# Queueing the routing stage of a transformer block behind the iterations of its local attention

## What is computed

```
xn   = layernorm(x)
s    = xn @ [q_route_tok, kv_route_tok]      # 2 rows of 2048 scores
for 20 rounds:                               # per row
    a = cur * (log k - logsumexp((s + b) / cur))
    b = -relu(s + a);  cur = max(0.7 * cur, 0.03)
idx_q, idx_kv = top_k(exp((s + a + b) / cur), 1024)
light = local_attention(layernorm(xn))       # 8 heads, windows of 64, look-around 1
heavy = attention(tokens idx_q over tokens idx_kv)
x = x + light + scatter(heavy, idx_q; null token elsewhere)
x = x + mixture_of_8_experts_top2(layernorm(x))
```

## Time and profile before

| | |
|---|---|
| median of 3 runs | 8584.27 us (8556.19 to 8604.47) |
| profiled execution | 8584.97 us |
| its span on the slowest core (core 4) | 8583.4 us |
| spans of the eight cores | 8517.4 to 8583.4 us |
| PE, DVE, ACT, POOL busy | 5417.4, 3297.1, 1409.5, 305.0 us |
| TensorE clock granted, mean of core 4 | 0.743 of full speed |

### The profile page before, as it was taken

The page is one execution under the profiler, slowest core; times in us unless marked ns, Lnnn a source line. Parts: engine busy times, 40 slices in busy tenths (PEclk is TensorE's granted clock), DMA queues, the critical chain, the costliest instruction groups (busy, mean ns, idle before and its releaser), DMA issues.

```text
span 8583.4 us, 70890 instructions; the slowest of 8 cores (8517.4 to 8583.4 us)
## 1 busy us (share of the span) xinstructions
PE 5417.4 (63%) x21893; PEld 2079.2 (24%) x22208; DVE 3297.1 (38%) x5936; ACT 1409.5 (16%) x1819; POOL 305.0 (4%) x335
## 2 busy tenths in 40 slices
PE   5220122245555445561698888888988888888887
PEld 1010000013333333310232332322323223232232
DVE  2733644484444444425332332333333333232232
ACT  1012000102222222210111111111111111111111
POOL 0022000000000000000000000000000000000000
PEclk8565555566555555575897998989989999897898
DMA  2110000010000000010211111112111020211110
GB/s 91 44 10 0 0 0 0 5 44 6 1 1 1 1 1 1 1 49 0 37 24 17 29 30 16 31 15 31 29 18 31 16 31 16 31 16 30 16 31 40
DMA packets 149539, 169.20 MB, mean 20 GB/s; under 512 B 55972, under 2 KB 125092, under 8 KB 142772
## 3 DMA queue, kind: packets, MB, share of 16 engines
q0 software_dynamic: 140512, 111.61, 8.8%
q1 hardware_dynamic: 8660, 53.04, 1.8%
HBM read 267.67 MB, written 8.39 MB: 32 GB/s over the span
## 4 chain that ended last, share of the span: by engine, by line
PE 43%; DVE 4%; issue 3%; ACT 1%; DMA 1%; POOL 0%; DVEq 0%; another core or an unknown queue 0%; ACTq 0%; PEldq 0%; POOLq 0%
PE pSIM L1341 22%; PE pSIM L1415 12%; PE pSIM L1346 4%; PE pMISC L1302 2%; DVE x L1438 2%; PE pMISC L1383 2%; PE pSIM L1421 1%; ACT gtmp L1365 1%; DVE gtmp L1370 1%; DVE gTq L1376 1%; DMA b3ce<-b3c 1%; DVE u2sb L1394 0%; PE pSIM L1324 0%; DVEq L155 0%; DVE u3sb L1320 0%
## 5 line engine op out<-in xcount | busy, mean ns | idle before, releaser
L1415 PE MATMUL pSIM<-gTq,w2b 128*128 128x512 bf16 x4001 | 1196.3, 444 | 320.2 <-DVE gTq L1376 224.7
L1438 DVE SCALAR_TENSOR_TENSOR x<-pSIM,x 128x512 f32<-128x512 f32 x1024 | 708.3, 692 | 787.2 <-PE pSIM L1415 430.1
L1341 PE MATMUL pSIM<-xl2T,w1b 128*128 128x512 bf16 x3984 | 987.2, 389 | 31.0 <-DVE u3sb L1320 24.6
L1341 PE MATMUL pSIM<-xl2T,w3b 128*128 128x512 bf16 x4010 | 976.0, 383 | 4.7 <-issue 0.8
L1370 DVE TENSOR_TENSOR gtmp<-gtmp,gtmp 128x512 bf16<-128x512 bf16 x512 | 217.8, 425 | 1891.1 <-ACT gtmp L1365 1891.1
L1356 ACT ACTIVATE gtmp<-pSIM,b1ce 128x512 bf16<-128x512 f32 x512 | 351.8, 687 | 2965.9 <-PE pSIM L1346 2949.1
L1415 PEld LDWEIGHTS pSIM<-gTq,w2b 128*128 128x128 bf16 x4096 | 386.4, 108 | 1050.7 <-issue 869.6
L969 PE MATMUL pT<-idbf,attnbf 128*128 128x128 bf16 x2048 | 258.7, 306 | 592.5 <-ACT attnbf L953 567.2
L1341 PEld LDWEIGHTS pSIM<-xl2T,w1b 128*128 128x128 bf16 x4096 | 364.8, 99 | 521.9 <-issue 186.2
L1341 PEld LDWEIGHTS pSIM<-xl2T,w3b 128*128 128x128 bf16 x4096 | 360.4, 98 | 488.2 <-issue 144.2
L1365 ACT ACTIVATE gtmp<-pSIM,b3ce 128x512 bf16<-128x512 f32 x512 | 352.0, 688 | 729.2 <-PE pSIM L1346 729.2
(11 more groups left out here) (262 smaller groups left out, 4781.3 us busy)
## 6 DMA issues: line engine op xcount, KB each, us to landing
w1b<-w1q POOLq DMA_DIRECT2D x32, 1024.0 KB, 10.1
w3b<-w3q POOLq DMA_DIRECT2D x32, 1024.0 KB, 14.3
w2b<-w2q POOLq DMA_DIRECT2D x32, 1024.0 KB, 17.1
xs<-xT SPq DMA_DIRECT2D x24, 1024.0 KB, 4.9
xc<-xT SPq DMA_DIRECT2D x16, 1024.0 KB, 4.9
out<-x SPq DMA_DIRECT2D x8, 1024.0 KB, 10.2
wst<-wqkv POOLq DMA_DIRECT2D x8, 256.0 KB, 4.1
cos<-cos SPq DMA_DIRECT2D x1, 1024.0 KB
```

Of the source, the lines that this page charges most:

```text
L1341: E.matmul(pSIM[:, 512 * bank:512 * bank + 512], wb[:, 512 * dc + 128 * hc:512 * dc + 128 * hc + 128], xl2T[:, 2048 * dc + 512 * tc: 2048 ...
L1415: ins = E.matmul(pch(yb), w2b[par][:, 1024 * hc + 128 * dc: 1024 * hc + 128 * dc + 128], gTq[:, 512 * hc:512 * hc + 512], start=(hc == 0), ...
L1438: E.scalar_tensor_tensor(x1[:, 2048 * dc + 512 * tc: 2048 * dc + 512 * tc + 512], pch(yb), 1.0, x1[:, 2048 * dc + 512 * tc: 2048 * dc + 51 ...
```

## The change

The block c1 goes. Its operations are recorded as before, but between `begin_stage` and `end_stage`, which keep them in lists of their own together with the order in which they were recorded over all engines. They have semaphores of their own (c1p, c1v, c1w, c1s, c1m, c1x). After iteration `it` of c2, `feed` appends recorded operations to the engines' lists until a share of (it + 1) / 72 of them is out, so the last go out after iteration 71. The recorded list has 398 operations. The two broadcasts go through the one bank of pMISC in four pieces of 512 columns (`c1bcast`), since pSIM is in use by c2. Four tiles that lay over lightT, which c2 writes, move to the area of ln2T: kbkv, cscr, u_rt, key_rt. Ahead of the next stage, four engines wait for all of c1's semaphores. In the list below the renamed semaphores of the other c1 operations are left out.

```diff
         self.q[eng].append((w, emit, None if inc is None else inc.h, k, pend))
+        if getattr(self, "_stage_on", False):
+            self.gseq.append(eng)
...
+    def begin_stage(self, ordmap):
+        self._saveq, self._saveord = self.q, self.ord
+        self.q = {e: [] for e in ENGS}
+        self.ord = ordmap
+        self.gseq = []
+        self._stage_on = True
+
+    def end_stage(self):
+        st = self.q
+        self.q, self.ord = self._saveq, self._saveord
+        self._stage_on = False
+        return [self.gseq, st, 0]
+
+    def feed(self, stage, frac):
+        gseq, st, done = stage
+        want = int(math.ceil(len(gseq) * min(1.0, frac)))
+        while done < want:
+            e = gseq[done]
+            self.q[e].append(st[e].pop(0))
+            done += 1
+        stage[2] = done
...
-    kbkv = sat("kbkv", [128, 2048], F32, LT)
-    cscr = sat("cscr", [128, 2048], F32, LT + 8192)
+    kbkv = sat("kbkv", [128, 2048], F32, BIG + 24576)
+    cscr = sat("cscr", [128, 2048], F32, BIG + 0)
...
-    u_rt = rowt("u_rt", 0, 0, 2, 2048, F32, LT)
-    key_rt = rowt("key_rt", 0, 0, 2, 2048, F32, LT + 8192)
+    u_rt = rowt("u_rt", 0, 0, 2, 2048, F32, BIG + 16384)
+    key_rt = rowt("key_rt", 0, 0, 2, 2048, F32, BIG + 8192)
...
+    def c1bcast(src_row, dst, wait=()):
+        b = _ap_base(src_row)
+        for tc in range(4):
+            P.do("tensor", (lambda b=b, tc=tc: lambda E:
+                            E.matmul(pMISC[:, 0:512], ones_f[b:b + 1, :],
+                                     src_row[:, 512 * tc:512 * tc + 512],
+                                     start=True, stop=True))(),
+                 waits=[(S["c1s"], S["c1s"].n),
+                        (S["c1w"], S["c1w"].n)] + list(wait),
+                 inc=S["c1m"])
+            P.do("scalar", (lambda dst=dst, tc=tc: lambda E:
+                            E.copy(dst[:, 512 * tc:512 * tc + 512],
+                                   pMISC[:, 0:512]))(),
+                 waits=[(S["c1m"], S["c1m"].n)], inc=S["c1s"], drain=True)
...
         P.do("gpsimd", lambda E: E.tensor_sub(u_rt, s_rt, rl_rt),
-             waits=[(S["scl"], S["scl"].n), (S["pool"], S["pool"].n)],
-             inc=S["pool"], drain=True)
+             waits=[(S["c1s"], S["c1s"].n), (S["c1p"], S["c1p"].n)],
+             inc=S["c1p"], drain=True)
...
-    P.flush("c1")
...
+    c1stage = P.end_stage()
 
     VC2 = S["vec"].n
     for it in range(128):
...
              waits=[(S["av"], S["av"].n)], inc=S["oe"], drain=True)
+        P.feed(c1stage, (it + 1) / 72.0)
+    P.feed(c1stage, 1.0)
+    assert not any(c1stage[1].values())
     P.flush("c2")
...
+    C1F = [(S[k], S[k].n) for k in ("c1p", "c1v", "c1w", "c1s", "c1m", "c1x")]
+    for _e in ("tensor", "vector", "scalar", "gpsimd"):
+        P.do(_e, lambda E: E.nop(), waits=C1F)
     P.do("vector", lambda E: E.tensor_mul(t_row, r_row, sr_row),
          inc=S["vec"], drain=True)
```

More of the change, by code:

```diff
@@ L350, in build @@
              "scl", "scl2", "pool", "sim", "mx", "ex", "tp", "tes", "tev",
-             "av", "rr", "rb", "oe", "fin"]
-    names += ["o_vector", "o_scalar", "o_gpsimd"]
+             "av", "rr", "rb", "oe", "fin",
+             "c1p", "c1v", "c1w", "c1s", "c1m", "c1x"]
+    names += ["o_vector", "o_scalar", "o_gpsimd",
+              "c1ov", "c1os", "c1og"]
     S = {k: Sem(nc, k) for k in names}
@@ L600, in build @@
         tap("lq", lq); tap("lk", lk); tap("vsh", vsh)
+    P.begin_stage({"vector": S["c1ov"], "scalar": S["c1os"],
+                   "gpsimd": S["c1og"]})
+    def c1bcast(src_row, dst, wait=()):
[12 more added lines that the diff above has]
+                 waits=[(S["c1m"], S["c1m"].n)], inc=S["c1s"], drain=True)
     P.do("gpsimd", lambda E: E.tensor_copy(rl_rt, s_rt),
-         waits=[(S["vec"], S["vec"].n)], inc=S["pool"], drain=True)
+         waits=[(S["vec"], S["vec"].n)], inc=S["c1p"], drain=True)
     cur_eps = 4.0
@@ L608, in build @@
         P.do("gpsimd", lambda E: E.tensor_sub(u_rt, s_rt, rl_rt),
-             waits=[(S["scl"], S["scl"].n), (S["pool"], S["pool"].n)],
-             inc=S["pool"], drain=True)
+             waits=[(S["c1s"], S["c1s"].n), (S["c1p"], S["c1p"].n)],
+             inc=S["c1p"], drain=True)
         P.do("vector", lambda E: E.reduce_max(sc_rt[:, 0:1], u_rt, axis=AX.X),
-             waits=[(S["pool"], S["pool"].n)], inc=S["vec"], drain=True)
+             waits=[(S["c1p"], S["c1p"].n)], inc=S["c1v"], drain=True)
         P.do("vector", (lambda inv=inv: lambda E:
@@ L630, in build @@
                                         ALU.mult, ALU.add))(),
-             inc=S["pool"], drain=True)
+             inc=S["c1p"], drain=True)
         P.do("scalar", lambda E: E.activation(rl_rt, s_rt, AF.Relu,
                                               bias=sc_rt[:, 5:6], scale=1.0),
-             waits=[(S["pool"], S["pool"].n)], inc=S["scl"], drain=True)
+             waits=[(S["c1p"], S["c1p"].n)], inc=S["c1s"], drain=True)
         cur_eps = max(cur_eps * 0.7, 0.03)
@@ L637, in build @@
                                              ALU.add, ALU.min),
-         waits=[(S["scl"], S["scl"].n)], inc=S["pool"], drain=True)
+         waits=[(S["c1s"], S["c1s"].n)], inc=S["c1p"], drain=True)
     P.do("gpsimd", lambda E: E.tensor_scalar(z_rt, key_rt, 0.0, None, ALU.is_equal),
-         inc=S["pool"], drain=True)
-    P.do("gpsimd", lambda E: E.memset(u_rt, 1.0), inc=S["pool"], drain=True)
+         inc=S["c1p"], drain=True)
+    P.do("gpsimd", lambda E: E.memset(u_rt, 1.0), inc=S["c1p"], drain=True)
     P.do("vector", lambda E: E.tensor_tensor_scan(zp_rt, u_rt, z_rt, 0.0,
                                                   ALU.mult, ALU.add),
[L644 to L647, removed]
+         waits=[(S["c1p"], S["c1p"].n)], inc=S["c1v"], drain=True)
+    P.do("vector", lambda E: E.tensor_sub(zp_rt, zp_rt, z_rt), inc=S["c1v"], drain=True)
+    P.do("vector", lambda E: E.tensor_mul(zp_rt, zp_rt, z_rt), inc=S["c1v"], drain=True)
+    c1bcast(key_rt[0:1, :], cmpw, wait=[(S["c1v"], S["c1v"].n)])
     for c in range(16):
@@ L651, in build @@
                                     key_rt[:, 128 * c:128 * c + 128], idf[0:2, 0:2]))(),
-             waits=[(S["vec"], S["vec"].n), (S["vec2"], S["vec2"].n),
-                    (S["scl"], S["scl"].n)],
-             inc=S["mm3"])
+             waits=[(S["c1s"], S["c1s"].n), (S["c1w"], S["c1w"].n)],
+             inc=S["c1m"])
         P.do("vector", (lambda c=c: lambda E:
                         E.tensor_copy(kcol[:, 2 * c:2 * c + 2], pMISC[0:128, 0:2]))(),
-             waits=[(S["mm3"], S["mm3"].n)], inc=S["vec2"], drain=True)
+             waits=[(S["c1m"], S["c1m"].n)], inc=S["c1w"], drain=True)
     for c in range(16):
@@ L661, in build @@
                                     idf[:, :]))(),
-             waits=[(S["vec2"], S["vec2"].n)], inc=S["mm3"])
+             waits=[(S["c1w"], S["c1w"].n)], inc=S["c1m"])
         P.do("vector", (lambda c=c: lambda E:
@@ L665, in build @@
                                       pMISC[0:1, 0:128]))(),
-             waits=[(S["mm3"], S["mm3"].n)], inc=S["vec2"], drain=True)
-    bcast(t_row, kbkv, wait=[(S["vec2"], S["vec2"].n)])
+             waits=[(S["c1m"], S["c1m"].n)], inc=S["c1w"], drain=True)
+    c1bcast(t_row, kbkv, wait=[(S["c1w"], S["c1w"].n)])
     for c in range(16):
@@ L674, in build @@
                                             ALU.is_gt))(),
-                 waits=[(S["vec2"], S["vec2"].n), (S["scl"], S["scl"].n)],
+                 waits=[(S["c1w"], S["c1w"].n), (S["c1s"], S["c1s"].n)],
                  drain=True)
@@ L684, in build @@
                                     idf[:, :]))(),
-             waits=[(S["mx"], S["mx"].n), (S["vec2"], S["vec2"].n)],
-             inc=S["mm3"])
+             waits=[(S["c1x"], S["c1x"].n), (S["c1w"], S["c1w"].n)],
+             inc=S["c1m"])
         P.do("vector", (lambda c=c: lambda E:
@@ L689, in build @@
                                       pMISC[0:2, 0:128]))(),
-             waits=[(S["mm3"], S["mm3"].n)], inc=S["vec2"], drain=True)
+             waits=[(S["c1m"], S["c1m"].n)], inc=S["c1w"], drain=True)
     P.do("vector", lambda E: E.tensor_add(rank_rt, rank_rt, zp_rt),
-         waits=[(S["vec2"], S["vec2"].n)], inc=S["vec"], drain=True)
+         waits=[(S["c1w"], S["c1w"].n)], inc=S["c1v"], drain=True)
     P.do("vector", lambda E: E.tensor_scalar(sel_rt, rank_rt, 1024.0, None, ALU.is_lt),
-         inc=S["vec"], drain=True)
+         inc=S["c1v"], drain=True)
     P.do("vector", lambda E: E.tensor_scalar(nmqbf[:, :], rank_rt[0:1, :], 1024.0,
                                              None, ALU.is_ge),
-         inc=S["vec"], drain=True)
+         inc=S["c1v"], drain=True)
     for c in range(16):
@@ L701, in build @@
                                     sel_rt[:, 128 * c:128 * c + 128], idf[0:2, 0:2]))(),
-             waits=[(S["vec"], S["vec"].n), (S["vec2"], S["vec2"].n)],
-             inc=S["mm3"])
```

(15 more changed lines are left out.)

12 lines of the change are left out of this document (6 added, 6 removed).

## The result

The changed kernel takes 8469.35 us (median) against 8587.11. Some executions of either kernel are a slower kind, with one die at a lower granted clock (0.70 against 0.75 in the worst), and the ratio is taken over the others: 0.9868, 95% interval 0.9841 to 0.9895, so some 113 us less (1.3%). The slowest core of the profiled execution is core 3 now (core 4 before).

What follows compares the result with a forecast made beforehand. No engine bounds c1 or c2; each is one serial chain hopping between engines. Three stretches, to 359.5, 778.3 and 1066 us, make a stage of about 1067 against 1192: 8585 - 125 = 8460 us, range 8425 to 8520.

Steps and rivals of the forecast that it cites:

- Part 1: The 20 scoring rounds of c1 beside iterations 0 to 32 of c2: 359.5 us, overlap taking 117 off.
- the walk: Batch-by-batch queue calculation for the 20 rounds, from start distances in the old timelines; iteration 33 starts at 359.5 us.
- the lock: Rival, chance 0.33: in seven batches the GpSimd subtract holds up DVE's scaling of lattnT; 17 us, total 8477.
- s: The GpSimd subtract in each of the 20 scoring rounds, 4.66 us to the next start; the operation itself lasts 4.48.
- much over 18: Sign of a wrong prediction: a scoring round, forecast to spread over 18 us instead of 15.2, takes much longer.
- near the lower end: Forecast's choice for the subtract disturbing DVE, between bounds of nothing and +90 us over twenty rounds.
- The rival's 7 x 2.5 us: Scaling of lattnT delayed by the GpSimd subtract in batches 5, 10, 15, 18, 23, 28, 31: 17 us; chance 0.33.
- Part 2: End of c1 beside iterations 33 to 71: 195.3 and 208.8 us add up, 404 us, reaching 778.3.
- Part 3: Iterations 72 to 127 of c2 alone: 56 x 5.14 = 287.8 us, reaching 1066.
- Reload: Rival, chance 0.06: ACT switches tables there and back in 33 batches of the merged block; 85 us, total 8545.
- no overlap: Rival, chance 0.04: c1 and c2 add up as before, less about 3 us; total 8582.
- slower: Rival, chance 0.05: the GpSimd subtract grows beside a working DVE; at three times its length, 8639.

Runs made afterwards that it cites:

- the PSUM form: Changed kernel, but the local-attention exponential writes float32 to idle pSIM banks, where sum and scaling read it; stage 1086.2 us against 1083.8.
- two iterations a round: Changed kernel with only the schedule altered: two local-attention iterations beside each of the 20 scoring rounds; stage 1054.2 us, ratio to before 0.9793.
- the gaps: Schedule with two iterations per round; from iteration 41 single routing operations go where DVE waits inside an iteration; stage 948.4 us, ratio to before 0.9739.

## Why the prediction was right, and what it missed

- *Two serial chains that share in-order queues gain only by what one does on other engines while the other holds DVE.* Right. Without overlap the stage is 1190.6 us; with it 1083.8.
- *Part 1, the walk.* Right in its steps and in the places of the meetings, short by the lock: the key operation at 376.2 against 359.4, and 18.7 us from one subtract to the next on average, where "much over 18" was to be a sign of a wrong prediction. The step that failed is the value taken for s, "near the lower end", which put nothing into the sum for it: s and an iteration's own DVE work do disturb each other, and that is worth 17 us. The rival's 7 x 2.5 us is nearly the same, in part by luck: the first iteration, which it doesn't have, costs about 2 us of the 17 (its batch ends 15.9 us after the start; 13.7 walked, 14.0 in the PSUM form), and its seven cost about 2.1 each. The PSUM form shows the lock by removal: 13.6 us go on this schedule, net of the dearer scalings, and 25 on that of two iterations a round. The Trainium skill (SBUF — State Buffer, Who interferes with whom) states this lock, between a GpSimd operation and a tensor_scalar in a two-port mode but not a reduction; the traces agree: 3.21 us for the scaling, 0.42 for the sum.
- *Part 2, the tail adds in full.* Right for this order of the queues: 692.8 us from scan to end against 691.9. TensorE's next scores do wait behind the batch's transposes (31.7 us over 95 iterations), as was said, and about as much comes back: the waits ahead of the four kinds of small copies out of pMISC fall from 49.8 us to 28.5 (the largest, kcol, is shown), and those ahead of the comparisons from 12.7 to 3.4.

```profile
L721 DVE TENSOR_REDUCE rankc<-cscr 128x1 f32<-128x2048 f32 x32 | 73.2, 2286 | 3.7 <-DVE cscr L715 0.5
L768 DVE SCALAR_TENSOR_TENSOR lsim<-pSIM,lmask 128x256 f32<-128x256 f32 x95 | 40.4, 425 | 40.8 <-PE pSIM L759 31.7 <-DVE kcol L699 0.7 <-DVE mtok L748 0.5
...
L715 DVE TENSOR_SCALAR cscr<-cmpw,kcol 128x2048 f32<-128x2048 f32 x16 | 20.6, 1286 | 1.7
...
L699 DVE COPY kcol<-pMISC 128x2 f32<-128x2 f32 x16 | 2.6, 160 | 6.3 <-PE pMISC L694 5.5 <-DVE lightT L819 0.2
```

  The same copy before:

```profile
L656 DVE COPY kcol<-pMISC 128x2 f32<-128x2 f32 x16 | 2.5, 159 | 18.6 <-PE pMISC L650 18.6
```

  The comparison pairs take what they took in the earlier trace rows. That this tail is dear only by its place is shown by the gaps: 106 us.
- *Part 3, tables, block boundary, tiles.* Right: 5.14 us an iteration at the end, one table load, 1.5 us for all the rest.
- *The time.* 8460 forecast, 8469 measured. The 17 us that the stage is short of its forecast are the lock, the first of the rivals, which stood at 8477. That the whole time lies as close to the forecast as to that rival is luck, since medians of this kernel move by as much as lies between; the stage, 1083.8 us against 1067 and 1084, decides it. By mechanism the rival is what happened, and its 0.33 should have been more than the 0.52 of the forecast: no row spoke for a POOL that is free beside DVE.
- *Reload, no overlap, slower.* None occurred. A subtract keeps 4.48 us beside a busy DVE; the one that waits is DVE.

## What to carry to other kernels

Where engines run their queues in order, a second chain that is queued behind whole iterations of a first gains only on the engines that they don't share; walk one period with the start distances of the two timelines, for every position that the batches can take, and the stage comes out within some microseconds (with one position walked for all, it was 26 us off). Put the guest's operations of the shared engine ahead of the instruction that waits, not behind the iteration: here that was worth as much (106 us of 8587) as the whole change. And before GpSimd work is laid under VectorE work, look for VectorE operations that scale from SBUF to SBUF: here each that began under a long GpSimd instruction ended only behind it. A way out that these runs show is to have the producer write to an idle PSUM bank and to scale from there, 0.17 us an iteration dearer, and needed only in the iterations that meet such an instruction.

## What the runs showed of the hardware

- A GpSimd subtract of 2 x 2048 float32 (4.48 us) holds up a DVE tensor_scalar of 128 x 256 bf16 from SBUF to SBUF until 0.07 to 0.09 us after its own end (0.29 us become up to 3.21; 4.58 under a longer GpSimd tensor_scalar of 7.17). It doesn't hold a reduction from SBUF (0.42), a reciprocal of one column, or copies and a tensor_scalar out of PSUM (0.28, 0.48). Two partitions on one side are enough.
- The same tensor_scalar from PSUM float32 takes 0.48 us against 0.29 from SBUF bf16.
- Exponential, logarithm, relu and copy of two interleaved stages are served by a single table load.
